# Output projection of the attention moved from the token tiles into the heads, in a transformer block on one core

## The chip, the core and the metric

The kernel runs on one core of a Trainium2 chip. The metric is the device time of one execution in microseconds; it is compared with the median of three runs of the kernel before, 3258.67 us (3257.95 to 3259.64).

## What is computed

The block has two halves, each behind a layernorm that is scaled and shifted per batch. Four batches of 2048 tokens with 512 channels; 16 heads of 32 channels, so 64 pairs of batch and head ("heads" below). In each head only the 409 queries with the largest norm attend; the output of all other tokens is zero in that head. Cut to what matters:

```
Q, K, V = proj(Wq, bq), proj(Wk, bk), proj(Wv, bv)      # 64 heads of 2048 x 32
_, top_idx = top_k(norm(Q), 409)
out_sel = softmax(Q[top_idx] @ K.T / sqrt(32)) @ V       # 409 x 32 per head
out_full = zeros(64, 2048, 32); out_full[:, top_idx] = out_sel
attn = reshape(out_full) @ Wo.T + bo                     # (4, 2048, 512)
x = x + ga * attn
h = layernorm(x) * (1 + cb) + sb
hq = fp4(h)                                              # blocks of 16: scale = max|h|/6, rounding to 8 levels
hid = fp4(silu(hq @ Wg.T) * (hq @ Wu.T))                 # 1408 wide
x = x + gb * (hid @ Wd.T)
```

`fp4` divides each block of 16 by its scale, rounds to the grid 0, 0.5, 1, 1.5, 2, 3, 4, 6 and multiplies by the scale again. Every product with a weight is done in three f16 matmuls (high by high, high by low, low by high), which keeps f32 accuracy.

## The kernel before

The program is written instruction by instruction: each engine (TensorE = PE, VectorE = DVE, ScalarE = ACT, GpSimd = POOL, SyncE = SP, which issues the plain DMAs) has its own list, executed in order, and semaphores tie the lists together. There are four stages: queries, keys and values (both before the change's main part), the attention (`attend`), and the feed-forward tiles (`feed_forward`).

**Attention.** `drive` runs 64 slots, one per head; the middle ones are a loop with two slots in its body. A slot has 8 steps k = 0..7. In every step PE computes the scores of 256 keys against 410 queries (`scores`, line 1614) into one pair of PSUM banks, ACT takes the exponential of them (`exponentials`, line 1517), and in the odd steps PE multiplies the exponentials of two earlier steps with the values (`weigh`, line 1625, f32). The next `scores` must wait for the exponential, since there is one pair of banks. Between them stand pieces for neighbouring heads: `scores_for_max` (line 1576) two heads ahead, whose maxima DVE takes (line 1412), `turn_queries` (line 1562), `rows`, `gather_last`, and `turn_output` for the head before. `divide` (DVE) divides by the sum of the exponentials, POOL's `scatter` adds the bias of the values and writes the 409 rows of 32 channels to DRAM with four indirect DMAs (`o_d`, line 1373), at the tokens' places. The rest of `o_d` is filled with zeros beforehand. POOL's list per head: cut the fetched queries, fetch the next ones (four indirect DMAs), scatter.

**Feed-forward.** 64 tiles of 128 tokens, one slot each, again a loop in the middle (four slots in its body). A slot t works on three tiles at once: the front of tile t+1 (attention output, residual, layernorm, `quantise_h`), the gate and up products of tile t (`gate_up`, three column chunks k of 512, 512 and 384, lines 2158 to 2160), and the down product of tile t-2 (`down`, lines 2180 to 2182). In the front, tile t+2 of `o_d` is turned (`turn_a`, 4 transposes, line 2131), split into a high and a low f16 part (`high_of_a` on ACT, `low_of_a` on DVE), and `attention_out` multiplies it with Wo in 12 matmuls (lines 2137 to 2139); `take_attention` (DVE) scales and adds `bo`. Then POOL does `residual` and `modulate`, DVE `moments`, `normalise`, `quantise_h`, POOL `scale_h`, and PE's `turn_x` (line 2146) turns the tile at the start of its slot into PSUM bank t0. ACT and DVE split it (`high_of_x`, `low_of_x`), which `gate_up` needs. `hidden` (DVE, line 1919) multiplies silu and up; `hidden_units` scales the 1408 columns to units of their blocks; `hidden_add` and `hidden_take` round by adding and subtracting a constant of the element's own exponent (`add_magic`: mask the exponent, `max(.,1)*ROUND`, add); POOL's `scale_hidden` and PE's `turn_hidden` (line 2170; its second chunk also uses bank t0) feed `down`.

**The seam.** The last heads and the first tiles are written out by hand in `last` and in the special cases `at(t, 0)` to `at(t, 2)` of the slots, and in POOL's list after its loop over the heads.

## Time and profile before

| | |
|---|---|
| median of three runs | 3258.67 us |
| the profiled execution, its own time | 3256.89 us |
| span of the profiled execution | 3255.0 us |
| busy: PE, DVE, ACT, POOL | 97%, 78%, 35%, 48% |
| mean granted PE clock | 0.989 of full speed |
| queries, keys and values | 0 to about 637 us |
| attention | about 637 to 1566 us |
| feed-forward | about 1566 us to the end |

The profile lists for one execution when each engine worked on what. The last 1.9 us of the execution's time lie outside the span. A busy PE row does not by itself show that PE is the limit, since matmuls overlap and their ends are modelled: what matters is the distance between the starts of neighbouring instructions, and whether an engine sat idle before one.

### The profile page before, as it was taken

To read this page: it belongs to the slowest core of one execution; us is meant where nothing else is said; L and a number is where in the kernel's file an instruction comes from. 1 tells how busy PE (TensorE), PEld (TensorE's weight loads), DVE (VectorE), ACT (ScalarE), POOL (GpSimd) and SP (SyncE) were. 2 spreads that over 40 slices of the span, in tenths; PEclk is the share of its full clock that TensorE was granted. 3 is DMA by queue.
4 is the path that set the end of the run, shared out by engine and by line. 5 is a ranking of instruction groups with operands and counts; after the bars stand their busy time and mean duration, and the time that the engine had idled before them with its cause. 6 is when DMAs were issued, how large, how long until landed. Compare 5 with 4: busy or idle time off the path is not lost.

```text
span 3255.0 us, 49640 instructions
## 1 busy us (share of the span) xinstructions
PE 3148.5 (97%) x16552; PEld 1459.3 (45%) x16552; DVE 2545.4 (78%) x3750; ACT 1141.7 (35%) x1588; POOL 1563.1 (48%) x1420
## 2 busy tenths in 40 slices
PE   7999999799999999999999999999999999999998
PEld 3543454333333333333455555555555555555554
DVE  4658976566666666666799989889999998899985
ACT  6853333366666666665211111111111111111111
POOL 3432224356666666663544444444444444444442
PEclk9999999899999999999999999999999999999999
DMA  6858849854333333324100010000000010000000
GB/s 237 285 174 250 220 137 251 204 174 142 86 103 106 86 116 95 84 78 126 42 30 30 29 32 32 29 31 30 29 29 29 32 32 29 30 31 29 29 20 17
DMA packets 238230, 290.81 MB, mean 89 GB/s; under 512 B 94648, under 2 KB 150328, under 8 KB 237384
## 3 DMA queue, kind: packets, MB, share of 16 engines
q1 hardware_dynamic: 221768, 283.07, 29.2%
q0 software_dynamic: 16384, 6.76, 1.0%
q8 instruction: 42, 0.69, 0.1%
q14 instruction: 36, 0.29, 0.0%
HBM read 169.36 MB, written 111.70 MB: 86 GB/s over the span
## 4 chain that ended last, share of the span: by engine, by line
PE 74%; ACT 2%; DVE 2%; issue 1%; POOL 1%; DMA 0%; SPq 0%; ACTq 0%; POOLq 0%; DVEq 0%
PE bank L1625 12%; PE pair L2158 9%; PE pair L2160 9%; PE pair L2159 9%; PE pair L1614 7%; PE pair L1576 5%; PE bank L2182 4%; PE bank L2180 4%; PE bank L2181 4%; ACT shared L1517 2%; PE pair L2137 2%; PE pair L2138 2%; PE pair L2139 2%; PE bank L2170 1%; PE pair L2170 1%
## 5 line engine op out<-in xcount | busy, mean ns | idle before, releaser
L1412 DVE TENSOR_REDUCE top<-pair 128x1 f32<-128x1024 f32 x378 | 451.0, 1221 | 219.2 <-PE pair L1576 219.2
L1517 ACT ACTIVATE shared<-pair,p_bias 128x820 f32<-128x820 f32 x512 | 483.3, 944 | 373.8 <-PE pair L1614 373.6
L2158 PE MATMUL pair<-gu,xT_hi 128*128 128x512 f16 (+1 forms) x1536 | 555.9, 362 | 4.1 <-DVE bridge L1919 2.1
L2160 PE MATMUL pair<-gu,xT_lo 128*128 128x512 f16 (+1 forms) x1536 | 555.8, 362 | 0.0
L2159 PE MATMUL pair<-gu,xT_hi 128*128 128x512 f16 (+1 forms) x1536 | 555.7, 362 | 0.0
L1625 PE MATMUL bank<-shared,bridge 128*33 128x410 f32 x2048 | 404.2, 516 | 0.0
L455 POOL DMA_INDIRECT q_sel<-q_d,chosen x256 | 247.3, 966 | 96.7 <-issue 80.6
L1614 PE MATMUL pair<-q_exp,bridge 98*128 98x410 f16 x1024 | 267.8, 343 | 25.9 <-ACT shared L1517 25.4
L1373 POOL DMA_INDIRECT o_d<-o_rows,chosen x256 | 250.1, 977 | 81.5 <-issue 64.2
L2180 PE MATMUL bank<-dn,bridge 128*128 128x512 f16 x704 | 268.4, 381 | 0.0
L2181 PE MATMUL bank<-dn,bridge 128*128 128x512 f16 x704 | 268.2, 381 | 0.0
L2182 PE MATMUL bank<-dn,bridge 128*128 128x512 f16 x704 | 267.9, 381 | 0.0
L2090 ACT ACTIVATE silu<-pair 128x512 f32<-128x512 f32 (+1 forms) x128 | 69.6, 544 | 510.7 <-PE pair L2160 510.7
L1576 PE MATMUL pair<-bridge,q_max 96*128 96x512 f16 x756 | 209.0, 386 | 17.6 <-DVEq L1458 15.2
L2160 PEld LDWEIGHTS pair<-gu,xT_lo 128*128 128x128 f16 x1536 | 150.4, 98 | 154.4 <-issue 0.8
L2158 PEld LDWEIGHTS pair<-gu,xT_hi 128*128 128x128 f16 x1536 | 150.4, 98 | 140.9 <-issue 4.0
L2159 PEld LDWEIGHTS pair<-gu,xT_hi 128*128 128x128 f16 x1536 | 150.4, 98 | 137.6 <-issue 0.8
L2021 POOL TENSOR_SCALAR f_rstd<-f_mv 128x1 f32<-128x1 f32 x64 | 87.0, 1359 | 219.4 <-DVE f_mv L1892 219.4
L2084 ACT ACTIVATE xT_hi<-pair 128x512 f16<-128x512 f32 x64 | 38.2, 597 | 437.6 <-PE pair L2146 437.6
L1625 PEld LDWEIGHTS bank<-shared,bridge 128*33 128x33 f32 x2048 | 98.1, 110 | 204.4 <-issue 204.1
L1614 PEld LDWEIGHTS pair<-q_exp,bridge 98*128 98x128 f16 x1024 | 64.4, 97 | 264.2 <-ACT shared L1517 233.0
L2038 POOL TENSOR_TENSOR bridge<-bridge,q_scale 128x1408 f32<-128x1408 f32 x64 | 165.8, 2590 | 24.8 <-DVE bridge L1804 17.5
(270 smaller groups left out, 6000.9 us busy)
## 6 DMA issues: line engine op xcount, KB each, us to landing
bridge<-k_d SPq DMA_DIRECT2D x384, 128.0 KB
v_d<-v SPq DMA_DIRECT2D x16, 1056.0 KB, 10.0
bridge<-v_d SPq DMA_DIRECT2D x64, 264.0 KB, 2.7
x<-in_x SPq DMA_DIRECT2D x16, 1024.0 KB, 8.8
q_d<-q SPq DMA_DIRECT2D x16, 1024.0 KB, 4.3
a_in<-o_d SPq DMA_DIRECT2D x64, 256.0 KB, 2.6
f_x<-in_x SPq DMA_DIRECT2D x64, 256.0 KB, 2.6
out<-shared SPq DMA_DIRECT2D x64, 256.0 KB, 2.0
```

The costliest lines, as they stand in the source:

```text
L1373: pool.indirect_dma_start(o_rows, bass.IndirectOffsetOnAxis(ap=con["chosen"][0:n, t, h:h + 1], axis=0), o_rows_of[u][0:n, t, :], None).the ...
L1412: ve.tensor_reduce(top[:, t, half:half + 1], ps[:, :, :].rearrange("p a n -> p (a n)"), AX.X, ALU.max, negate=True).then_inc(max_done, 1)
L1517: act.activation(p32[k % PB][:, :, :], ps_exp[:, :, 0:NQ], ACT.Exp, bias=con["p_bias"][:, 0:1], scale=scale).then_inc(p_done, 1)
L1576: last = pe.matmul(ps[:, s, :], q_max[u][:, t * P:(t + 1) * P], k_max[u][:, at:at + 512], start=True, stop=True)
L1614: last = pe.matmul(ps_exp[:, s, 0:NQ], k_exp[u][:, at:at + P], q_exp[u][:, :], start=True, stop=True)
L1625: last = pe.matmul(ps_out[at:at + VCOLS, 0:NQ], v_tok[u][:, t, :], p32[k % PB][:, s, :], start=k == 0, stop=k == STEPS - 1)
L2158: pe.matmul(o, xT_hi[:, c, :], w_hi[:, c, c0:c0 + n], start=c == 0, stop=False)
L2159: pe.matmul(o, xT_hi[:, c, :], w_lo[:, c, c0:c0 + n], start=False, stop=False)
L2160: last = pe.matmul(o, xT_lo[:, c, :], w_hi[:, c, c0:c0 + n], start=False, stop=c == KC - 1)
L2180: pe.matmul(ps_d[:, :], hT_hi[:, c, :], w_hi[:, c, :], start=c == 0, stop=False)
L2181: pe.matmul(ps_d[:, :], hT_hi[:, c, :], w_lo[:, c, :], start=False, stop=False)
L2182: last = pe.matmul(ps_d[:, :], hT_lo[:, c, :], w_hi[:, c, :], start=False, stop=c == FC - 1)
```

## The change

The projection with Wo is done per head. Since Wo acts on a head's 32 channels alone, the 409 rows of a head times 32 rows of Wo give 409 rows of 512 channels that are added to the tokens' rows. In each attention slot there are now:

- on DVE, behind the division: the bias of the values (scaled), the split into f16 parts side by side (`o_split`, 96 columns: high, low, high);
- on PE, `turn_back` (four transposes by matmul, into 96 x 410) at step 2, two slots behind the head's own; DVE copies it to SBUF (`take_back`);
- on PE, `project`: four matmuls, one for each 128 queries, at steps 5 and 7 (two heads back) and 1 and 3 (three heads back), 96 rows (high, low, high) against `wo_head` (high, high, low of Wo's rows), 512 columns;
- on ACT, `take_rows`: the 128 x 512 result is scaled into `o_tile`;
- on POOL, `scatter`: four indirect DMAs per head that add (compute_op add) rows of 512 channels, 2 KB each, to `o_d`. The rows of two heads can meet in one token, so the first DMA of a head waits until all of the head before have landed. POOL's scatter stands two heads later in its list than before. `o_d` is filled with `bo` instead of zeros.
- on SP, three loads of `wo_head` and one of the head's bias per head.

In the feed-forward `turn_a`, `high_of_a`, `low_of_a`, `attention_out` and `take_attention` are gone; `residual` reads `a_in` directly. The block scales are computed with a two-input instruction (a constant tile `least` as second input) in place of one with two constants. For the hidden units the mask of the exponents moves to the end of `hidden_units`, ACT multiplies by ROUND (`magic`), and `max` goes into the instructions that add and subtract. `turn_x(t+1)` stands inside `down(t-2)` and `low_of_x(t+1)` at the end of DVE's slot. The down weights lie where `o_tile` is, so they are loaded after the last scatter.

The diff, cut to its core:

```diff
@@ attend
+    BACK_AT = 2
+    PROJECT_AT = {5: (-2, 0, False), 7: (-2, 1, True), 1: (-3, 2, True), 3: (-3, 3, False)}
...
                 def scatter(h):
-                    u = h % 2
-                    pool.wait_ge(o_divided, h + 1)
-                    pool.tensor_tensor(o_rows_of[u][:, :, :], o_rows_of[u][:, :, :],
-                                       early["bv"][:, h % H * HD:(h % H + 1) * HD].unsqueeze(1).to_broadcast([P, QT, HD]),
-                                       ALU.add).then_inc(o_biased, 1)
...
                     for t in range(QT):
                         n = rows_of(t, TOP)
-                        pool.indirect_dma_start(o_rows, bass.IndirectOffsetOnAxis(ap=con["chosen"][0:n, t, h:h + 1], axis=0),
-                                                o_rows_of[u][0:n, t, :], None).then_inc(o_stored[u], 16)
+                        pool.wait_ge(o_taken, h * QT + t + 1)
+                        if t == 0:
+                            for k in range(QT):
+                                need(pool, o_stored[k], 16 * h)
+                            if h % H == 0:
+                                pool.wait_ge(o_zeroed, 16 * (L // N) * (h // H + 1))
+                        pool.indirect_dma_start(o_rows, bass.IndirectOffsetOnAxis(ap=token[0:n, t, h:h + 1], axis=0),
+                                                o_tile[h % 2][t][0:n, :], None, compute_op=ALU.add).then_inc(o_stored[t], 16)
...
-                    if h >= 4:
-                        scatter(h - 4)
+                    if h >= 6:
+                        scatter(h - 6)
...
+                def take_back(h, u, bank):
+                    ve.wait_ge(o_back, h + 1)
+                    need(ve, o_proj, h * QT - QT)
+                    ve.tensor_copy(oT[u][:, :], bank[0:KROWS, 0:NQ]).then_inc(o_back_taken, 1)
...
+                    ve.tensor_tensor(o_div[:, :, :], o_div[:, :, :], bv_head[u][:, :].unsqueeze(1).to_broadcast([P, QT, HD]),
+                                     ALU.add).then_inc(o_step, 1)
...
+                    ve.tensor_copy(o_split[:, :, :].rearrange("p t (k r) -> p t k r", k=3)[:, :, 0:3:2, :],
+                                   o_div[:, :, :].unsqueeze(2).to_broadcast([P, QT, 2, HD])).then_inc(o_step, 1)
...
+                    ve.tensor_tensor(o_split[:, :, HD:2 * HD], o_div[:, :, :], o_split[:, :, 0:HD], ALU.subtract).then_inc(o_cut, 1)
...
+                def take_rows(h, u, t, bank):
+                    n = rows_of(t, TOP)
+                    act.wait_ge(o_proj, h * QT + t + 1)
+                    need(act, o_stored[t], h * 16 - 16)
+                    act.activation(o_tile[u][t][0:n, :], bank[0:n, :], ACT.Copy, scale=1.0 / (W_UP * O_UP)).then_inc(o_taken, 1)
...
+                def project(h, u, t, bank, loaded, taken):
...
+                    need(pe, o_taken, taken)
+                    pe.matmul(bank[0:n, :], oT[u][:, t * P:t * P + n], wo_head[u][:, :], start=True, stop=True).then_inc(o_proj, 1)
@@ feed_forward
-        ve.tensor_scalar(sc[:, :], am[:, :], 1.0 / 6.0, 1e-12, ALU.mult, ALU.max).then_inc(step, 1)
+        ve.scalar_tensor_tensor(out=sc[:, :], in0=am[:, :], scalar=1.0 / 6.0, in1=least[:, 0:nb], op0=ALU.mult,
+                                op1=ALU.max).then_inc(step, 1)
...
+            ve.tensor_scalar(mg2[:, :].bitcast(I32), xn2[:, :].bitcast(I32), EXP_BITS, None, ALU.bitwise_and).then_inc(q2_step, 1)
...
         def hidden_add(t):
-            add_magic(ve, t, xn2, mg2, q2_step)
+            ve.wait_ge(q2_step, t * QS + 6)
+            ve.scalar_tensor_tensor(out=xn2[:, :], in0=mg2[:, :], scalar=ROUND, in1=xn2[:, :], op0=ALU.max, op1=ALU.add)\
+              .then_inc(q2_step, 1)
...
+        def magic(t):
+            act.wait_ge(q2_step, t * QS + 5)
+            act.activation(mg2[:, :], mg2[:, :], ACT.Copy, scale=ROUND).then_inc(q2_step, 1)
...
-        def attention_out(t):
-            pe.wait_ge(a_lo, t + 1)
-            for c in range(KC):
-                pe.matmul(ps_w[:, :], aT_hi[:, c, :], wo_hi[:, c, :], start=c == 0, stop=False)
-                pe.matmul(ps_w[:, :], aT_hi[:, c, :], wo_lo[:, c, :], start=False, stop=False)
-                last = pe.matmul(ps_w[:, :], aT_lo[:, c, :], wo_hi[:, c, :], start=False, stop=c == KC - 1)
-            last.then_inc(w_ready, 1)
...
-        def down(t):
+        def down(t, turn=None):
...
             for k, (c0, n) in enumerate(T2_CHUNKS):
+                if k == 2 and turn is not None:
+                    turn_x(turn)
```

What it moves, at two places. First PE's list in a middle slot of the attention, steps 0 to 3 (`q_exp` are the scores, `shared` the exponentials in `weigh`, `q_max` the scores for the maxima, `q_split` the turned queries). Before:

```order
L1614 MATMUL pair<-q_exp,bridge 128x410 x2
L1562 MATMUL bank<-ident,q_split 96x128 x3
L1562 MATMUL bank<-ident,q_split 96x26
L1576 MATMUL pair<-bridge,q_max 128x512 x4
L1614 MATMUL pair<-q_exp,bridge 128x410 x2
L1625 MATMUL bank<-shared,bridge 33x410 x4
L1614 MATMUL pair<-q_exp,bridge 128x410 x2
L1576 MATMUL pair<-bridge,q_max 128x512 x2
L1580 MATMUL pair<-bridge,q_max 26x512 x4
L1614 MATMUL pair<-q_exp,bridge 128x410 x2
L1625 MATMUL bank<-shared,bridge 33x410 x4
```

The same place after, from step 1 on:

```order
L1671 MATMUL pair<-q_exp,bridge 128x410 x2
L1682 MATMUL bank<-shared,bridge 33x410 x2
L1714 MATMUL bank<-wo_head,oT 128x512
L1682 MATMUL bank<-shared,bridge 33x410 x2
L1671 MATMUL pair<-q_exp,bridge 128x410 x2
L1631 MATMUL pair<-bridge,q_max 128x512 x2
L1635 MATMUL pair<-bridge,q_max 26x512 x4
L1704 MATMUL bank<-ident,o_split 96x128 x3
L1704 MATMUL bank<-ident,o_split 96x26
L1671 MATMUL pair<-q_exp,bridge 128x410 x2
L1714 MATMUL pair<-wo_head,oT 25x512
L1682 MATMUL bank<-shared,bridge 33x410 x4
```

Step 1 has one projection between the two halves of `weigh`, step 3 one (of only 25 queries) in front of it, and `turn_back` stands at the end of step 2. Steps 5 and 7 are like 3 and 1, with 128 queries each.

Second, DVE's list in a feed-forward slot, from `hidden` of the second chunk to the first instructions of the next slot (`q_amax` to `q_xn` are `quantise_h` or, with `bridge`, `hidden_units`; rows of the same kind within `quantise_h` are left out on both sides). Before:

```order
L1919 SCALAR_TENSOR_TENSOR bridge<-pair,silu 128x384
L1782 TENSOR_REDUCE q_amax<-bridge 128x88
L1785 TENSOR_SCALAR q_scale<-q_amax 128x88
L1787 RECIPROCAL q_inv<-q_scale 128x88
L1789 SCALAR_TENSOR_TENSOR bridge<-bridge,q_inv 128x1408
L1933 SCALAR_TENSOR_TENSOR bridge<-bank,shared 128x512
L1872 TENSOR_TENSOR xT_lo<-pair,xT_hi 128x512
L1925 SCALAR_TENSOR_TENSOR bridge<-bank,bridge 128x512
```

After:

```order
L2017 SCALAR_TENSOR_TENSOR bridge<-pair,silu 128x384
L1885 TENSOR_REDUCE q_amax<-bridge 128x88
L1888 SCALAR_TENSOR_TENSOR q_scale<-q_amax,f_least 128x88
L1891 RECIPROCAL q_inv<-q_scale 128x88
L1893 SCALAR_TENSOR_TENSOR bridge<-bridge,q_inv 128x1408
L2002 TENSOR_SCALAR bridge<-bridge 128x1408
L1975 TENSOR_TENSOR xT_lo<-pair,xT_hi 128x512
L2031 SCALAR_TENSOR_TENSOR bridge<-bank,shared 128x512
L2023 SCALAR_TENSOR_TENSOR bridge<-bank,bridge 128x512
```

The mask of the exponents (line 2002) now stands ahead of `low_of_x` (line 1975), and `low_of_x` ahead of `take_down` (line 2031).

## Rows read from the trace of the kernel before

**Rows 1.** Length; busy PE, PEld, DVE, ACT, POOL; PE clock, DMA share, GB/s.
```profile
1000.00:1400.00 400.00, 389.81 (x2181) 132.98 (x2178) 272.07 (x476) 246.94 (x307) 251.04 (x308) 1.00 0.34 95
1800.00:2200.00 400.00, 400.00 (x2093) 209.91 (x2091) 359.90 (x447) 65.22 (x123) 192.83 (x140) 1.00 0.09 30
```
**Rows 2.** Timeline of PE in a feed-forward slot: start, duration, line, idle in brackets.
```profile
1997.74 0.60 PE L2146 MATMUL pair<-ident,q_xq 128*128 128x128 f32 x4
1998.18 0.60 PE L2170 MATMUL bank<-ident,bridge 128*128 128x128 f32 x4
1998.62 0.38 PE L2137 MATMUL pair<-wo_hi,aT_hi 128*128 128x512 f16 x1
...
2001.20 0.60 PE L2170 MATMUL pair<-ident,bridge 128*128 128x128 f32 x4
...
2012.33 0.60 PE L2131 MATMUL pair<-ident,a_in 128*128 128x128 f32 x4
...
2016.67 0.38 PE L2180 MATMUL bank<-dn,bridge 128*128 128x512 f16 x1
...
2023.79 0.60 PE L2146 MATMUL pair<-ident,q_xq 128*128 128x128 f32 x4
```
**Rows 3.** Timeline of PE in an attention slot.
```profile
1015.43 0.52 PE L1614 MATMUL pair<-q_exp,bridge 98*128 98x410 f16 x2
...
1016.20 1.04 PE L1576 MATMUL pair<-bridge,q_max 96*128 96x512 f16 x4
1017.07 0.52 PE L1614 MATMUL pair<-q_exp,bridge 98*128 98x410 f16 x2
1017.52 1.57 PE L1625 MATMUL bank<-shared,bridge 128*33 128x410 f32 x8
1019.03 0.52 PE L1614 MATMUL pair<-q_exp,bridge 98*128 98x410 f16 x2
...
1020.66 0.52 PE L1614 MATMUL pair<-q_exp,bridge 98*128 98x410 f16 x2 [0.35 <-ACT shared L1517]
...
1029.76 0.52 PE L1614 MATMUL pair<-q_exp,bridge 98*128 98x410 f16 x2
```
**Rows 4.** ACT grouped by line: count | busy us, mean ns | idle before, releasers.
```profile
L1517 ACT ACTIVATE shared<-pair,p_bias 128x820 f32<-128x820 f32 x512 | 483.3, 944 | 373.8 <-PE pair L1614 373.6
...
L1066 ACT ACTIVATE v<-mm 128x512 f32<-128x512 f32 x64 | 38.0, 604 | 92.3 <-PE mm L1100 70.1 <-DMA v_d<-v 22.0
```
**Rows 5.** Timeline of ACT: a copy of 1408 columns.
```profile
615.02 1.37 ACT L1045 ACTIVATE f_row_hi<-f_quant 128x1408 f16<-128x1408 f32 x1
```
**Rows 6.** Timeline of DVE in a feed-forward slot.
```profile
2004.55 1.84 DVE L1798 TENSOR_SCALAR bridge<-bridge 128x1408 f32<-128x1408 f32 x1
...
2013.16 0.69 DVE L1919 SCALAR_TENSOR_TENSOR bridge<-pair,shared 128x512 f32<-128x512 f32 x1 [0.24 <-ACT shared L2090]
2013.77 0.68 DVE L1877 SCALAR_TENSOR_TENSOR aT_lo<-pair,aT_hi 128x512 f16<-128x512 f32 x1
2014.92 0.69 DVE L1782 TENSOR_REDUCE q_amax<-f_h 128x32 f32<-128x512 f32 x1 [0.47 <-POOL f_h L2027]
2015.64 1.83 DVE L1785 TENSOR_SCALAR q_scale<-q_amax 128x32 f32<-128x32 f32 x1
...
2020.88 0.55 DVE L1919 SCALAR_TENSOR_TENSOR bridge<-pair,silu 128x384 f32<-128x384 f32 x1
...
2023.11 0.20 DVE L1785 TENSOR_SCALAR q_scale<-q_amax 128x88 f32<-128x88 f32 x1
...
2025.63 0.68 DVE L1933 SCALAR_TENSOR_TENSOR bridge<-bank,shared 128x512 f32<-128x512 f32 x1
```
**Rows 7.** Timeline of DVE near the end: the mask of 1408 columns while POOL rests.
```profile
3200.61 0.88 DVE L1796 TENSOR_SCALAR bridge<-bridge 128x1408 int32<-128x1408 int32 x1
```
**Rows 8.** Timeline of POOL: the second and the fourth scatter DMA of a head.
```profile
1028.31 0.98 POOL L1373 DMA_INDIRECT o_d<-o_rows,chosen  x1 [0.30 <-issue]
...
1030.87 0.93 POOL L1373 DMA_INDIRECT o_d<-o_rows,chosen  x1 [0.30 <-issue]
```

More of the change, by code:

```diff
@@ L1856, in run @@
             load_a(2, 2)
-            drive(sp, slot, last, scattered)
+            drive(sp, slot, last)
             for u in range(2):
@@ L1960, in slot @@
                 ve.wait_ge(vec_in["gb"], 16)
-            else:
-                low_of_x(t)
             if has(t, -2):
                 low_of_hidden(t - 2, 0)
-            if has(t, 1):
-                take_attention(t + 1)
             if has(t, -2):
@@ L1986, in slot @@
             hidden_units(t)
+            if has(t, 1):
+                low_of_x(t + 1)
             if has(t, -2):
@@ L2000, in run @@
             drive(ve, slot, last)
-        return low_of_a, take_attention, moments, normalise, quantise_h, low_of_x, run
+        return hidden, moments, normalise, quantise_h, low_of_x, run
     def gpsimd(pool):
@@ L2209, in slot @@
             gate_up(t, 1)
-            if has(t, 2):
-                turn_a(t + 2, t4 + 2)
             gate_up(t, 2)
             if has(t, -2):
-                down(t - 2)
+                down(t - 2, t + 1 if has(t, 1) else None)
         def last():
```

335 lines of the change are left out of this document (195 added, 140 removed).

## Prediction, before the changed kernel was run

> **What bounds the kernel now.** I read the busy times by stage first. In the feed-forward stretch PE is busy 400.00 of 400 us and DVE 359.90; in the attention stretch PE 389.81, DVE 272.07, ACT 246.94, POOL 251.04 [rows 1]. The granted clock is 1.00 of full speed (2.4 GHz) in both, so it can give nothing back. Since a busy row is no proof, I then read PE's timeline. A feed-forward slot goes from 1997.74 to 2023.79, 26.05 us, with no idle time in brackets [rows 2]: the distance between starts is PE's own work. An attention slot goes from 1015.43 to 1029.76, 14.33 us [rows 3]. Its odd steps are PE's work too: scores at 1017.07, next scores at 1019.03, 1.96 us, without a gap. Its even steps take 1.64 (1015.43 to 1017.07; 1019.03 to 1020.66), and one of them ends in 0.35 us in which PE waits for ACT's exponential [rows 3], which takes 0.94 [rows 4]. So in both stages time is counted in matmuls on PE, save for small slack in the even steps.
>
> **What the feed-forward loses.** `turn_a` is 1997.74 to 1998.18 by its twin `turn_x`, 0.44 us. `attention_out` is 1998.62 to 2001.20, 2.58 us for 12 matmuls, 0.215 each [rows 2]. 3.02 us per tile, 64 tiles: **-194**. All of it was PE time without a wait, so all of it is gained as long as no other engine becomes late.
>
> By the Trainium skill, "TensorE: Matmul & The Clock Gate", section "Back-to-back issue gap", a stream of weight loads and 512-column matmuls sustains some 131 ns each. By that, an estimate, the twelve would be 1.6 us and the saving 64 x 2.0 = 129. Here the starts stand 0.215 us apart, so the trace does not agree, and the sum goes by the rows.
>
> **Is DVE late then?** DVE is the one near its limit: 359.90 of 400 is 23.4 us of the 26.05, and the new slot would be 26.05 - 3.02 = 23.03. It loses `take_attention` and `low_of_a` (0.68 each by its row), the 1408-column multiplication by ROUND (1.84), and `max` costs nothing extra. The scale instruction takes 1.83 for 32 columns where the same form on 88 takes 0.20 [rows 6]; the long one looks like waiting for something else, not like work. I take the two-input form at 0.24 with its distance. Together that is 4.8 us less, so DVE has 18.6 us of work in 23.0. What counts is the order, so I follow one chain. PE ends the gate and up products of the second chunk at 2012.33 [rows 2]; DVE's `hidden` starts 0.83 later, at 2013.16, `low_of_a` (now gone) at 2013.77. `quantise_h` takes 2014.92 to 2020.88, 5.96; without the slow scale (1.87 start to start, of which 0.24 stay) 4.33. `hidden` of the third chunk and `hidden_units` take 2020.88 to 2025.63, 4.75 [rows 6]; the mask, which needs their result, starts about 0.12 later than a free instruction would and costs 0.88 [rows 7], of which about 0.08 lie beside the next; `low_of_x` costs 0.68 by `low_of_a`, with 0.06 for its wait. Sum from PE's end of the second chunk: 0.83 + 0.61 + 4.33 + 4.87 + 0.80 + 0.74 = 12.18 us. PE meanwhile has: third chunk 2012.33 to 2016.67 less `turn_a` 0.44, 3.90; `down` 2016.67 to 2023.79, 7.12 [rows 2]; `turn_x` inside it 0.44, the first `turn_hidden` 0.44. Sum 11.90. Then the second `turn_hidden` needs bank t0, which `low_of_x` frees. So PE waits about 0.3 us per tile: slot 23.3; over some 61 tiles **+18**. Bounds: nothing, if DVE's overlaps are a little better; and the mask at twice its price (it shares its place with POOL's long instructions in the middle of the stage, while rows 7 shows it with POOL at rest) adds 0.9 per tile, 55 us.
>
> ACT's multiplication by ROUND has its nearest row in a copy of 1408 columns, 1.37 us [rows 5]. It runs behind the mask while DVE does `low_of_x` and the next slot's first work, and ACT is busy 65.22 of 400 us [rows 1], so it is hidden. Were it not, it would cost 1.37 a tile, 88 us, less the 0.68 of `low_of_x` beside it.
>
> **What the attention gains in work.** `project` is four matmuls of 512 moving columns, as `scores_for_max` is: 1016.20 to 1017.07 for four, 0.87 [rows 3]. They stand in the odd steps, where PE has no slack, so 0.87 per slot is the least. Three of them stand beside the f32 `weigh`; two scores of 410 columns would be 0.2175 x 410 / 512 x 2 = 0.35, but `weigh` starts 0.45 behind them (1017.07 to 1017.52) [rows 3], so I add 0.09 for each new change of type: 1.13 per slot. `turn_back` is four transposes, about 0.44 by `turn_x`, at step 2, where PE idles 0.35 [rows 3]: up to 0.1 is left over. `take_rows` is a copy of 128x512 out of PSUM, 604 ns [rows 4], four per slot; ACT has 246.94 / 400 x 14.33 = 8.85 us of work in a slot and gets 11.3 in 15.5. DVE has 9.75 and gets four small instructions (at most 0.68 each), 12.5. No engine passes PE. Sum 1.13 to 1.2 per slot, some 62 slots: **+72**. Bounds: 54 (0.87 each, nothing else) and, if each projection also delays the exponentials that a scores matmul waits for, 1.6, 100.
>
> **The scatter.** A scatter DMA is 0.98 on POOL, and one of 25 rows 0.93, each with 0.30 before it [rows 8]: the price hardly knows the rows, so I take 1.28 for rows of 2 KB that add, too. POOL has 251.04 / 400 x 14.33 = 9.0 us busy a slot and eight gaps of 0.30, 11.4; without the scatters 6.3, without the bias add too about 6. So a slot of 15.5 leaves 2.3 us for each scatter DMA. The transfers move 409 x 2 KB = 0.84 MB a slot; if adding means reading too, 2.5 MB at three passes. 95 GB/s are 0.34 of the engines' time [rows 1], so full would be 279 GB/s: 9.0 us more beside today's 4.9, 13.9 of 15.5. It fits, not by much.
>
> **The seam.** POOL's scatter stands two heads later, so behind the loop there are eight more scatter DMAs in front of the first tiles' residuals: 8 x 1.28 [rows 8], **+10**. Bounds 5 (half of it beside PE's last steps) and 30 (the landing of the last additions must be awaited before `a_in` and before the down weights come in). The first slot's fewer DMAs and the last tile's shorter tail change 1 or 2 us, against each other.
>
> **Sum** against the profiled execution: 3256.9 - 194 + 18 + 72 + 10 = 3163. The median of the runs is 1.8 above that execution, so **3164** us; 2.9% faster.
>
> **The rivals.**
>
> *The feed-forward slot follows DVE's chain.* For it: 12.18 against 11.90 is already on the wrong side, and each tenth that DVE loses there (a quantisation that comes later since POOL's `modulate` comes later, a mask beside POOL) is PE's. In the worst order `quantise_h` ends as late after the third chunk as now, 2020.88 - 2016.67 = 4.2 us; then units, mask and `low_of_x` follow, 4.2 + 4.87 + 0.80 + 0.74 = 10.6 against 7.12 + 0.88 = 8.0 of PE: 2.6 per tile, 157 us in place of 18. Against it: the 1.83 scale was the main lateness. Time 3200 to 3300. Chance 0.15.
>
> *The attention's slot is longer than its matmuls.* In the odd steps ACT now has the exponential and a 0.60 copy, 1.55 of 1.96; if the copy starts just ahead of the next exponential, scores, exponential and copy form a ring, and each of four steps gains up to 0.3 more. 16.2 us a slot, +0.75 x 62: about 3210. Chance 0.13.
>
> *The other side: the adding scatter.* One mechanism: a scatter DMA costs POOL, or its landing before the next head's first, more than the slot has. At s us for one, the slot is 6 + 4 s. Attention becomes limiting at s = 2.3; the kernel is slower than before when the slot takes about 17.1, since -194 + 18 + 10 = -166 over 62 slots is 2.7 more than 14.33: s = 2.8, or a head's additions landing over 12 us. At s = 3.0 the slot is 18.0: 3257 - 166 + 62 x 3.7 = 3320. For it: no row shows a DMA that adds, and 128 descriptors of 2 KB stand where 128 bytes were. Against it: 0.98 against 0.93. Chance 0.06.
>
> A page of the Trainium skill, "DMA: Bandwidth & Descriptors", section "Anatomy of one DMA", gives about 2.0 us and bytes / 436e3: 2.6 us to the landing of a 256 KB scatter, an estimate, which would fit between heads; no row of this case shows an adding one.
>
> *The adopted sum*, with its small terms off by a little: 0.64. The last 0.02: gains and losses cancel.
>
> **Range and chances.** The sum's own range: the DVE term 0 to 55, attention 54 to 100, seam 5 to 30, 3131 to 3225 at the extremes, which do not come together; with the rivals at 3200 to 3210 inside and what the saved DVE time may give beyond, 3128 to 3218 for 8 in 10. What a measurement can tell from no change is 0.2%, 6.5 us. Faster 0.92, same 0.02, slower 0.06.
>
> **What would show it.** Feed-forward slots of 23.3 us from `turn_x` to `turn_x`, with some 0.3 us of idle PE ahead of the second `turn_hidden`, released by DVE's `low_of_x`; no PE wait there means the mask is cheap. The scale at 0.2 instead of 1.83. Attention slots of 15.5, PE gap-free in the odd steps, `turn_back` in the old 0.35 gap; POOL scatter rows near 1.0. The prediction is wrong where a scatter row is over 2 us, or where PE's wait in a feed-forward slot is over 1 us.

## The result, and the profile after

The changed kernel takes 3300.71 us (median of 4 runs, 3296.10 to 3301.42), the kernel before in the same comparison 3259.01: ratio 1.0125, 95% interval 1.0108 to 1.0143. It is 1.3% slower where 2.9% faster was forecast. The profiled execution has a span of 3298.2 us, 43.2 more than before.

The busy times of the same two stretches as [rows 1]:

```profile
1000.00:1400.00 400.00, 399.76 (x2182) 133.91 (x2179) 281.51 (x534) 279.15 (x381) 279.89 (x255) 1.00 0.72 147
1800.00:2200.00 400.00, 374.94 (x1909) 191.59 (x1908) 323.09 (x415) 79.64 (x127) 208.62 (x143) 0.99 0.10 32
```

From the page, the shares of the chain that ended last, and the group of the adding scatters (count, busy us, mean ns, idle before):

```profile
PE 42%; DVE 22%; POOL 8%; issue 6%; DMA 1%; ACT 1%; POOLq 0%; DVEq 0%; SPq 0%; ACTq 0%
...
L1394 POOL DMA_INDIRECT o_d<-dn,token x256 | 400.8, 1566 | 251.1 <-ACT dn L1564 182.8
```

In the attention PE has no idle time left: 399.76 of 400. In the feed-forward, where PE was busy 400 of 400, it now idles 25 us in 400, and DVE's share of the last chain, 2% before, is 22%.

The starts of PE's own landmarks in both timelines divide the span (us):

| part | before | after | difference | forecast |
|---|---|---|---|---|
| to the first scores of the attention | 640.3 | 642.3 | +2.1 | 0 |
| to its last scores | 923.9 | 1013.0 | +89.1 | +72 |
| to the fourth `turn_x` | 68.9 | 77.6 | +8.7 | +10, less some 9 of saved work |
| 60 feed-forward slots | 1562.4 | 1506.2 | -56.2 | -164 |
| from the last `turn_x` to the end | 59.6 | 59.1 | -0.5 | some -3 |

The forecast's -194 + 18 is 2.74 us for each of the 60 slots and the rest in the first and last tiles. The slots' miss, 108 us, is four fifths of the whole miss of 137 us (43 slower in place of 94 faster).

PE's timeline in a feed-forward slot, the counterpart of [rows 2]:

```profile
1998.89 0.33 PE L2236 MATMUL pair<-gu,xT_hi 128*128 128x384 f16 x1
...
2007.97 0.61 PE L2224 MATMUL pair<-ident,q_xq 128*128 128x128 f32 x4
...
2010.36 0.60 PE L2248 MATMUL bank<-ident,bridge 128*128 128x128 f32 x4
2012.94 1.08 PE L2248 MATMUL pair<-ident,bridge 128*128 128x128 f32 x4 [1.98 <-DVE xT_lo L1975]
2013.82 0.63 PE L2236 MATMUL pair<-gu,xT_hi 128*128 128x512 f16 x1
2014.24 0.63 PE L2237 MATMUL pair<-gu,xT_hi 128*128 128x512 f16 x1
...
2016.62 0.38 PE L2237 MATMUL pair<-gu,xT_hi 128*128 128x512 f16 x1
2016.84 0.38 PE L2238 MATMUL pair<-gu,xT_lo 128*128 128x512 f16 x1
```

From the end of the second chunk's products, 1998.89, to where the second `turn_hidden` could start, 2010.36 + 0.44, PE needs 11.91 us: the forecast's 11.90. But it starts at 2012.94, released by `low_of_x`, after PE has rested 1.98 us and not 0.3. Behind this stop the matmuls start 0.43 apart in place of 0.22. The granted clock there:

```profile
2005.00:2010.00 5.00, 5.00 (x27) 2.47 (x26) 4.79 (x8) 0.60 (x1) 1.06 (x1) 1.00 0.00 0
2013.00:2016.00 3.00, 3.00 (x10) 1.56 (x11) 2.27 (x4) 1.67 (x3) 2.44 (x2) 0.50 0.00 0
```

0.50 is the lower of its two levels, 1.2 GHz, after some 2 us of rest; 2012.94 to 2016.38 then costs about 1.7 us more. It happens in 12 of the 60 slots, behind rests of 1.95 to 1.98 us; in 36 others PE rests 1.73 to 1.98 us (once 0.87) and the granted clock stays at 1.00.

DVE's and POOL's timelines of the same stretch, in order of time:

```profile
2000.43 2.59 POOL L2132 TENSOR_TENSOR bridge<-bridge,q_scale 128x1408 f32<-128x1408 f32 x1
2000.51 0.69 DVE L1885 TENSOR_REDUCE q_amax<-f_h 128x32 f32<-128x512 f32 x1
2001.23 1.84 DVE L1888 SCALAR_TENSOR_TENSOR q_scale<-q_amax,f_least 128x32 f32<-128x32 f32 x1
...
2012.20 0.68 DVE L1975 TENSOR_TENSOR xT_lo<-pair,xT_hi 128x512 f16<-128x512 f32 x1
...
2015.42 2.11 DVE L2006 SCALAR_TENSOR_TENSOR bridge<-bridge 128x1408 f32<-128x1408 f32 x1
2016.13 2.53 POOL L2111 TENSOR_TENSOR shared<-f_x,bridge 128x512 f32<-128x512 f32 x1
...
2018.70 0.69 DVE L1980 BATCH_NORM_STATS2 f_stats<-shared 128x6 f32<-128x512 f32 x1 [1.16 <-POOL shared L2111]
...
2025.45 2.59 POOL L2132 TENSOR_TENSOR bridge<-bridge,q_scale 128x1408 f32<-128x1408 f32 x1
...
2027.95 0.19 DVE L1888 SCALAR_TENSOR_TENSOR q_scale<-q_amax,f_least 128x32 f32<-128x32 f32 x1
```

The scale of 32 columns takes 1.84 us in its new two-input form as in the old one (1.83, [rows 6]), and ends at 2003.07, where POOL's multiplication of 1408 columns ends (2003.02). In the next slot it comes later, has 0.09 us in common with the same POOL instruction, and takes 0.19. The reduction between them lies wholly inside POOL's instruction and takes its plain 0.69. So one kind of DVE instruction waits for POOL and another does not. POOL waits as well: its addition at 2016.13 (1.26 where DVE leaves it alone) takes 2.53 and ends 1.1 after DVE's `hidden_add` (the row at 2015.42). The Trainium skill, "SBUF — State Buffer", section "Who interferes with whom", says which: a DVE instruction with two inputs in SBUF excludes a POOL instruction that reads SBUF, and so does a `tensor_scalar` in a mode that uses both ports; a reduction does not. By that rule the new form of the scale cannot help, since it trades one reason for the other. These rows agree for the scale, the reduction and POOL's addition; the prediction did not weigh it.

An attention slot on PE, the counterpart of [rows 3]:

```profile
1022.67 0.52 PE L1671 MATMUL pair<-q_exp,bridge 98*128 98x410 f16 x2
1023.12 0.88 PE L1682 MATMUL bank<-shared,bridge 128*33 128x410 f32 x4
1023.93 0.39 PE L1714 MATMUL bank<-wo_head,oT 96*128 96x512 f16 x1
1024.25 0.88 PE L1682 MATMUL bank<-shared,bridge 128*33 128x410 f32 x4
1025.07 0.52 PE L1671 MATMUL pair<-q_exp,bridge 98*128 98x410 f16 x2
...
1026.28 0.51 PE L1704 MATMUL bank<-ident,o_split 128*96 128x128 f16 x4
1026.72 0.52 PE L1671 MATMUL pair<-q_exp,bridge 98*128 98x410 f16 x2
1027.17 0.39 PE L1714 MATMUL pair<-wo_head,oT 96*25 96x512 f16 x1
1027.49 1.57 PE L1682 MATMUL bank<-shared,bridge 128*33 128x410 f32 x8
1028.99 0.52 PE L1671 MATMUL pair<-q_exp,bridge 98*128 98x410 f16 x2
```

Step 1 takes 2.40 us (1.96 before): the projection 0.32, and the split `weigh` 0.81 + 0.82 in place of 1.51. `turn_back` sits where PE had idled, and its step is 1.65. The slot is 15.77, without a wait.

### The profile page after: what moved, and what is told of

It reads as the page before. It is cut to its first block, busy times and chain, and to the rows that moved or that the text cites. A ratio compares the mean times of both kernels' runs of the same rounds, so it can differ in the third digit from the quotient of the medians.

```text
span 3298.2 us, 50101 instructions
## 1 busy us (share of the span) xinstructions
PE 3110.1 (94%) x16040; PEld 1392.6 (42%) x16040; DVE 2429.2 (74%) x3815; ACT 1329.3 (40%) x1844; POOL 1737.4 (53%) x1357
## 4 chain that ended last, share of the span: by engine, by line
PE 42%; DVE 22%; POOL 8%; issue 6%; DMA 1%; ACT 1%; POOLq 0%; DVEq 0%; SPq 0%; ACTq 0%
PE bank L1682 12%; PE pair L1671 7%; PE pair L1631 5%; DVE q_amax L1885 4%; PE pair L2238 4%; PE pair L2236 4%; PE pair L2237 4%; DVE q_scale L1888 3%; DVE bridge L1893 3%; DVE q_inv L1891 2%; DVE bridge L2017 1%; DVE q_xn L1893 1%; DVE q_xn L1904 1%; POOL f_rstd L2115 1%; POOL f_h L2119 1%
## 5 line engine op out<-in xcount | busy, mean ns | idle before, releaser
L2236 PE MATMUL pair<-gu,xT_hi 128*128 128x512 f16 (+1 forms) x1536 | 564.6, 368 | 4.1 <-DVE bridge L2017 2.3
L2237 PE MATMUL pair<-gu,xT_hi 128*128 128x512 f16 (+1 forms) x1536 | 564.5, 368 | 0.0
L2238 PE MATMUL pair<-gu,xT_lo 128*128 128x512 f16 (+1 forms) x1536 | 563.9, 367 | 0.0
L1394 POOL DMA_INDIRECT o_d<-dn,token x256 | 400.8, 1566 | 251.1 <-ACT dn L1564 182.8
L1682 PE MATMUL bank<-shared,bridge 128*33 128x410 f32 x2048 | 429.9, 520 | 0.0
L1631 PE MATMUL pair<-bridge,q_max 96*128 96x512 f16 x756 | 219.4, 386 | 18.0 <-DVEq L1493 15.2
L2126 POOL TENSOR_TENSOR q_xq<-q_xn,q_scale 128x512 f32<-128x512 f32 x64 | 68.3, 1068 | 230.5 <-DVE q_xn L1908 230.5
L1682 PEld LDWEIGHTS bank<-shared,bridge 128*33 128x33 f32 x2048 | 87.0, 110 | 169.6 <-issue 141.7
```

Of the source, the lines that this page charges most:

```text
L1394: pool.indirect_dma_start(o_rows, bass.IndirectOffsetOnAxis(ap=token[0:n, t, h:h + 1], axis=0), o_tile[h % 2][t][0:n, :], None, compute_op ...
L1631: last = pe.matmul(ps[:, s, :], q_max[u][:, t * P:(t + 1) * P], k_max[u][:, at:at + 512], start=True, stop=True)
L1682: last = pe.matmul(ps_out[at:at + VCOLS, 0:NQ], v_tok[u][:, t, :], p32[k % PB][:, s, :], start=k == 0, stop=k == STEPS - 1)
L2236: pe.matmul(o, xT_hi[:, c, :], w_hi[:, c, c0:c0 + n], start=c == 0, stop=False)
L2237: pe.matmul(o, xT_hi[:, c, :], w_lo[:, c, c0:c0 + n], start=False, stop=False)
L2238: last = pe.matmul(o, xT_lo[:, c, :], w_hi[:, c, c0:c0 + n], start=False, stop=c == KC - 1)
```

## Experiments

All but the thirteenth, which is the kernel before, are edits of the changed kernel. They ran in five groups, each on another chip and each beside the kernel before: it took 3258 us in runs 1 to 4 and 17 to 18, 3328 in 5 to 8, 3327 in 9 to 12 and 3289 in 13 to 16. The changed kernel itself was timed again only in the third and fourth group. Runs 1 to 4, 17 and 18 are therefore set against its first 3300.71 us, which is sound in so far as the kernel before took the same there within 1.2 us; all other times are compared within their group. A "stop" below is a rest of PE of more than 1 us in the attention; slots without one can be compared across the groups.

**1. The old form of the scale.**

```diff
-        ve.scalar_tensor_tensor(out=sc[:, :], in0=am[:, :], scalar=1.0 / 6.0, in1=least[:, 0:nb], op0=ALU.mult,
-                                op1=ALU.max).then_inc(step, 1)
+        ve.tensor_scalar(sc[:, :], am[:, :], 1.0 / 6.0, 1e-12, ALU.mult, ALU.max).then_inc(step, 1)
```

> One edit to the changed kernel: the block scales are computed again by the one-input instruction with two constants (line 1888). Theory A: in the feed-forward DVE and POOL cannot both use what they share, so the scale of 32 columns waits inside itself until POOL's multiplication of 1408 columns (line 2132) is over, whatever its form, as both forms have a second way into SBUF: its rows stay at 1.8 us in the slots where they overlap, 0.2 where they do not, and the time stays at 3300 us within 6. Rival B: the two-input form changed something after all (it removed a wait elsewhere, as its use in the change suggests): then the time rises by 10 us or more.

3292.95 us (3291.11 to 3293.92), ratio 1.0105 (1.0088 to 1.0122). The scale's rows are 1.83 or 0.18 as before, the slot 25.06 on average against 25.10. The form changes nothing in the wait. The 8 us are 2 more than I allowed; the slots give 60 x 0.04 = 2.5 of them, so that the old form is if anything the better one, and where the others come from was not followed.

**2. Maxima and inverse scales in PSUM.**

```diff
+    am1p, in1p = (banks[0][:, 0, k * (D // BLK):(k + 1) * (D // BLK)] for k in range(2))
...
-            block_units(ve, t, D, h, am1, sc1, in1, xn1, q1_step, lambda: need(ve, q1_done, t))
+            am, inv = (am1, in1) if isinstance(t, int) and t < 4 else (am1p, in1p)
+            block_units(ve, t, D, h, am, sc1, inv, xn1, q1_step, lambda: need(ve, q1_done, t))
```

> One edit to the changed kernel: for the tokens' tiles from the fifth on, the block maxima (input of the scale) and the inverse scales (input of the product) of quantise_h lie in PSUM, in a bank that is free in this stage. So the scale and the product have one input in SBUF in place of two. Theory A (the second SBUF input is what collides with POOL): the scale takes 0.2 us instead of 1.84 everywhere, the chain to low_of_x is 1.1 to 1.6 us shorter per tile, slots of 23.6 to 24.0 instead of 25.1 on average, time about 3235 us (3215 to 3250). Rival B (the instruction waits for POOL for another reason, its output or its place): 1.84 stays, and the time stays within 6 us of 3300.

3216.39 us (3215.58 to 3218.27), ratio 0.9872 (0.9856 to 0.9889): 84 us less than the changed kernel, 1.3% faster than the kernel before, and inside the 3215 to 3250 of theory A. DVE and POOL, in order of time:

```profile
2009.88 2.59 POOL L2134 TENSOR_TENSOR bridge<-bridge,q_scale 128x1408 f32<-128x1408 f32 x1
...
2010.71 0.19 DVE L1889 SCALAR_TENSOR_TENSOR q_scale<-pair,f_least 128x32 f32<-128x32 f32 x1
2010.93 0.36 DVE L1892 RECIPROCAL pair<-q_scale 128x32 f32<-128x32 f32 x1
2011.33 0.69 DVE L1894 SCALAR_TENSOR_TENSOR q_xn<-f_h,pair 128x512 f32<-128x512 f32 x1
2012.05 0.70 DVE L1901 TENSOR_SCALAR q_magic<-q_xn 128x512 int32<-128x512 int32 x1
```

Scale, reciprocal and product now run inside POOL's instruction (to 2012.47) at 0.19, 0.36 and 0.69. The first that waits is the mask at 2012.05 (0.70 in place of 0.43), a `tensor_scalar` with one input and one constant. The slot is 23.77, 1.33 less; 60 x 1.33 = 80 of the 84. This edit takes the collision away without touching the amount of work, and it carries the case: for the two-input form the wait is the second input from SBUF, not the instruction, its size or its output, which still lies in SBUF.

**3. `low_of_x` ahead of the mask.**

```diff
             hidden_units(t)
             if has(t, 1):
                 low_of_x(t + 1)
+            hidden_mask(t)
```

(`hidden_mask` is the instruction that ended `hidden_units`.)

> One edit to the changed kernel: low_of_x stands ahead of the mask of the exponents on DVE instead of behind it. Theory A (PE's wait of 1.98 us ends with DVE's chain, in which the mask is 0.8): the wait before the second turn_hidden falls to about 1.2, slots 0.6 to 0.8 shorter, time 3301 - 60 x 0.7 = about 3259 us (3250 to 3270). Rival C (what comes behind is set by ACT's multiplication, which now starts 0.6 later, and pushes everything that it pushes back): no gain, 3295 to 3310.

3293.44 us (3291.54 to 3295.40), ratio 1.0111 (1.0094 to 1.0128). PE's wait for `low_of_x` falls to 1.06, and a new wait of 0.36 to 0.50 for POOL's `scale_h` stands ahead of `turn_x`; the slot is 25.04. Theory A's gain (3250 to 3270 us) did not come: rival C, that something pushes back, is right in kind, and the time is 1.6 us under its 3295.

**4. `low_of_x` inside `hidden_units`.**

```diff
+        if between is not None:
+            between()
         ve.wait_ge(step, done[2])
         ve.scalar_tensor_tensor(out=blocks(xn[:, :]), in0=blocks(src[:, :]), scalar=sign * TIE_DOWN,
```

> One edit to the changed kernel: low_of_x stands inside hidden_units, behind the reciprocal and ahead of the product of 1408 columns. Theory A: the chain to low_of_x loses 1.62 of the product and 0.89 of the mask, 2.5 us, more than PE's wait of 1.98; PE waits no longer, no drop of its clock follows, and the slot is PE's own work, 23.05 to 23.4: time 3301 - 60 x 1.9 = about 3190 us (3180 to 3205). Rival C (the next lateness, ACT's multiplication or DVE's total work, takes over): slots of 24 or more, 3230 and above.

3289.82 us (3288.40 to 3290.17), ratio 1.0098 (1.0081 to 1.0115). Theory A's 3190 did not come, rival C's slot of 24 or more did. PE's wait for `low_of_x` is gone altogether, and the slot is 24.97: in its place PE waits 1.14 us for `hidden` and 0.36 to 0.50 for POOL's `scale_h`. DVE's timeline shows what sets the slot then:

```profile
1963.76 0.69 DVE L2025 SCALAR_TENSOR_TENSOR bridge<-bank,bridge 128x512 f16<-128x512 f32 x1 [1.33 <-ACT bridge L2184]
...
1967.74 0.69 DVE L1982 BATCH_NORM_STATS2 f_stats<-x 128x6 f32<-128x512 f32 x1 [1.16 <-POOL x L2111]
...
1971.05 0.55 DVE L1988 TENSOR_SCALAR f_h<-x,f_mv,f_rstd 128x512 f32<-128x512 f32 x1 [0.77 <-POOL f_rstd L2117]
...
1974.54 0.69 DVE L1885 TENSOR_REDUCE q_amax<-f_h 128x32 f32<-128x512 f32 x1 [1.28 <-POOL f_h L2121]
1975.26 1.84 DVE L1888 SCALAR_TENSOR_TENSOR q_scale<-q_amax,f_least 128x32 f32<-128x32 f32 x1
```

DVE waits once for ACT and three times for POOL, and POOL's work there waits for DVE: a ring, that is waits of engines for each other that close from slot to slot, of 25 us beside the one through PE. Two limits lay 0.1 us apart, so undoing the first alone gives next to nothing; that the second experiment gives 80 us fits, since the wait of the scale lies in both.

**5 and 6. Both edits; then the second ring shortened.** The fifth is 2 and 4 together. The sixth adds two moves: POOL's multiplication by `ga` ahead of `result`, and ACT's splits ahead of its multiplication by ROUND.

```diff
+            if has(t, 1):
+                gain(t + 1, t4 + 1, b1)
             if has(t, -3):
                 result(t - 3, t4 + 1)
             if has(t, 1):
-                residual(t + 1, t4 + 1, b1)
+                add(t + 1, t4 + 1)
...
-            if not at(t, 1):
-                magic(t - 1)
             if has(t, -2):
                 high_of_hidden(t - 2, 0)
                 high_of_hidden(t - 2, 1)
+            if not at(t, 1):
+                magic(t - 1)
```

> The edits of the second and the fourth experiment together (maxima and inverse scales in PSUM, low_of_x inside hidden_units). Theory D, formed from the fourth: two rings of nearly the same length bound the feed-forward slot, PE with DVE's chain to low_of_x (25.1 us in the changed kernel) and DVE with POOL and ACT (24.9 to 25.0: waits of 1.33 for ACT, 1.16 and 0.77 and 1.28 for POOL, and 1.84 in the scale). PSUM takes 1.4 from both, the move takes 2.5 from the first alone: slots of 23.5, by 0.2 to 0.3 better than the second experiment's 23.77, about 3200 us (3190 to 3208). Rival: the gains of the two add up, 84 + 11, for 3206 or more, as if there were no rings; or PE's own 23.05 is reached, 3172.

> The fifth with the second ring shortened: POOL multiplies the attention by ga ahead of the result of tile t-3 instead of behind it, and ACT splits the hidden units' two chunks ahead of its multiplication by ROUND. Theory D: the waits of DVE for ACT (1.33) and for POOL's residual (1.16) shrink, the slot falls from 23.5 to PE's own 23.1: about 25 us less than the fifth, 3175 us (3165 to 3185). Rival: DVE's hidden_add and POOL's addition still exclude one another, so the residual is not earlier and the slot stays within 0.1 of the fifth's.

3382.18 us (ratio 1.0171, 1.0140 to 1.0202) and 3315.06 us (0.9956, 0.9938 to 0.9974), on a chip with a slower attention (below). The feed-forward's slots are 24.10 and 23.02. The fifth's is longer than the second's 23.77 where theory D had it 0.2 to 0.3 shorter: with the scale repaired, moving `low_of_x` forward costs 0.33 a slot. The trace shows where: `low_of_x` now stands ahead of the mask, so ACT's multiplication and its splits come later, and DVE waits 1.33 us for the splits where it waits 0.73 in the second run. So there are two rings, as theory D has it, but the second one was taken too short by 0.6. The sixth is 67 us under the fifth where 25 was expected, because the fifth was longer; its slot is the forecast one. PE is busy there without a gap, at the 23.03 that the prediction worked out as PE's own work. Of the two waits that its edit was to shrink, the one for ACT is gone, and the one for POOL's residual is still 1.17; what each of its two moves gives alone was not run.

**7. Projections ahead of `weigh`.** At steps 1 and 7 `project_in_turn` stands ahead of both halves.

```diff
                         if k == 1 and has(i, -1):
+                            project_in_turn(i, u, k)
                             weigh(i - 1, 1 - u, STEPS - 2, None)
-                            project_in_turn(i, u, k)
                             weigh(i - 1, 1 - u, STEPS - 1, None)
```

> One edit to the changed kernel: the projections of steps 1 and 7 stand ahead of both halves of weigh (between f16 and f32 matmuls once) instead of between them. Theory E: each f32 matmul behind an f16 one costs some 0.1 us more, so the two steps lose 0.2 each: slots of 15.35 instead of 15.77, time lower by 25 us (15 to 30), 3275. Rival: the projection then waits for ACT's copy out of the same bank, and step and time stay as they are within 6 us.

3458.71 us (ratio 1.0394, 1.0374 to 1.0413). The changed kernel has no time in this group, so the time tells nothing alone; the attention's slots without a stop, of which there are four, are 15.36 to 15.42 against 15.77. The expected slot of 15.35 came.

**8. Scatters that write instead of adding.** `compute_op` is left out.

> One edit to the changed kernel: the scatter DMAs write instead of adding, so that each token keeps only the last head's rows (the sum over heads is left out). It prices the adding: if 1.57 us on POOL (1.0 before) comes from adding, the rows fall to 1.0; if it comes from rows of 2 KB, they stay at 1.5 to 1.6. In either case the time stays within 6 us of 3300, since PE has no wait in the attention; only the seam, where the second of two heads waits 3.7 us for the landing of the one before, may give 1 to 3 us.

One execution: 3388.11 us beside 3328 for the kernel before. POOL's rows, grouped by line:

```profile
L1394 POOL DMA_INDIRECT o_d<-dn,token x256 | 253.2, 989 | 487.1 <-ACT dn L1564 443.3 <-issue 24.8 <-DMA vec_sb<-mod_d 12.7
```

0.99 us: rows of 2 KB cost POOL no more than rows of 128 B, adding costs 0.58. From 1000 to 1400 us the packets of the queue for the indirect DMAs took 41.4% of the DMA engines for 22.37 MB in the changed kernel and 14.8% for 20.49 MB here, 2.6 times less per byte. The attention has stops without the adding too, but it is shorter: 1106.1 us against 1160.2 and 1164.7 in the fifth and sixth run on the same chip, which have the changed kernel's attention. Only 1 to 3 us, in the seam, had been expected.

**9 to 12. The same kernels beside the changed one.** The ninth is the changed kernel, the tenth the sixth, the eleventh the sixth with the seventh's edit; the twelfth is the eleventh with `scale_h(2)` moved between the last two scatters.

```diff
                 scatter(BH - 2)
+                f_scale_h(2)
                 scatter(BH - 1)
```

> The changed kernel without an edit, beside the next three and the kernel before on one chip: in the last call the attention's slots were 17 to 20 us long in some and 15.4 or 15.8 in others, on a chip where the kernel before took 3328 us as well, so the times of that call cannot be set against those of the first. If the chip is like the first: 3300 us, attention slots of 15.77, feed-forward slots of 25.10 on average.

> The sixth experiment again (maxima and inverse scales in PSUM, low_of_x inside hidden_units, multiplication by ga ahead of the result, ACT's splits ahead of its multiplication). Feed-forward slots of 23.02 without any wait of PE, as the sixth showed: 60 slots less 2.08 each are 125 us under the changed kernel, 3175 us (3168 to 3182).

> The tenth and the seventh together: the projections of steps 1 and 7 ahead of weigh as well. The seventh's undisturbed slots were 15.36 to 15.42 against 15.77: 0.4 x 61 = 24 us under the tenth, 3151 us (3145 to 3160). If the rival of the seventh holds (a wait for ACT's copy takes the place): within 6 us of the tenth.

> The eleventh with one step of the seam moved: POOL scales tile 2 (scale_h(2)) between the scatters of the last two heads instead of behind both. In the changed kernel PE waits 5.6 us for it and then 1.5 us for the hidden units' scale, which stays behind the last scatter. Theory F: the first wait goes and comes back in part as the second, net 1.5 to 5 us: 3148 us; rival: the load of f_x, for which POOL waits 8.8 us just behind, ends last anyway, and nothing changes.

3447.59, 3317.71, 3335.83 and 3337.58 us; ratios 1.0369 (1.0338 to 1.0399), 0.9964 (0.9950 to 0.9979), 1.0031 (1.0013 to 1.0050), 1.0042 (1.0015 to 1.0069). Tenth less ninth: -130 (expected -125). Eleventh less tenth: +18, where -24 was expected. In the twelfth PE's first wait, 6.5 us in the eleventh, is gone, and the second has grown from 1.47 to 5.74: the three slots of the seam took 72.2 us against 72.7, which is nearly the rival's nothing. (In the changed kernel's first trace PE's two waits are 5.58 and 1.47.) PE's timeline in the ninth's attention shows the stops:

```profile
1217.34 0.52 PE L1671 MATMUL pair<-q_exp,bridge 98*128 98x410 f16 x2
...
1218.54 0.60 PE L1631 MATMUL pair<-bridge,q_max 96*128 96x512 f16 x2
1220.20 2.36 DVE L1439 TENSOR_REDUCE top<-pair 128x1 f32<-128x1024 f32 x2 [3.12 <-PE pair L1631]
1220.23 0.94 ACT L1552 ACTIVATE shared<-pair,p_bias 128x820 f32<-128x820 f32 x1 [3.00 <-remote]
1221.23 0.53 PE L1671 MATMUL pair<-q_exp,bridge 98*128 98x410 f16 x2 [2.09 <-ACT shared L1552]
```

ACT's exponential, for which PE waits, starts at 1220.23 after 3.00 us of rest, and DVE's next reduction at 1220.20 after 3.12, both with their matmuls long started. The slots are 15.8 to 21 us long (one 22.7), and in heads 8 to 60 step 0 takes 3.5 us on average in place of 1.64, step 1 2.9 in place of 2.4.

The busy times of the whole attention, in the changed kernel's first trace and in the ninth (columns as in [rows 1]):

```profile
642.30:1655.30 1013.00, 1002.86 (x5429) 334.62 (x5428) 706.50 (x1334) 695.97 (x944) 677.93 (x620) 0.99 0.71 148
642.20:1797.10 1154.90, 1053.20 (x5428) 337.44 (x5426) 707.82 (x1334) 692.86 (x944) 678.03 (x620) 0.96 0.64 130
```

Of the 142 us more, PE rests 92. The other 50 are busy time for the same number of matmuls, at a mean granted clock of 0.96 in place of 0.99: many of the stops are followed by a stretch at half clock.

**13 to 16. Where the kernel before loses there.**

> The kernel before without an edit, for its trace on this chip. If the chip is like the first: 3259 us, attention slots of 14.33, feed-forward slots of 26.05. If it is like that of the last two calls: 3327 us, with all of the 70 us in the attention, as stops of about 2 us in every second slot, and the feed-forward at 26.05; rival: the loss is spread over the stages.

> The changed kernel without an edit, as the measure of the two beside it: 3300 us on a chip like the first, 3448 on one like the second.

> The kernel of the sixth and tenth runs (the ring shortened, feed-forward slots of 23.02): 125 us under the changed kernel on either chip, 3175 on the first, 3318 on the second.

> The kernel of the eleventh run (projections of steps 1 and 7 ahead of weigh as well): on a chip like the first 24 us under the fifteenth, 3151 us; on one like the second again some 15 us above it, since there the stops, not PE's work, set the slot.

3288.93, 3410.77, 3289.38 and 3316.60 us, against 3288.82 for the kernel before; ratios of the last three 1.0374 (1.0343 to 1.0406), 1.0006 (0.9994 to 1.0018), 1.0090 (1.0060 to 1.0120). Fifteenth less fourteenth: -121 (expected -125). Sixteenth less fifteenth: +27 (expected some +15). The kernel before loses all of it in the attention: 955.2 us from its first to its last scores against 923.9 on the first chip, in steps 1 and 6 (2.17 and 1.91 on average against 1.96 and 1.68), as smaller and more frequent rests than I expected. 27 of its 31 us more are rests of PE, and its mean granted clock there stays at 0.99. The changed kernel's attention takes 1124.7 there against 1013.0: 76 us more of rest, and a clock of 0.97.

**17 and 18. The two best kernels, on a chip like the first.**

> The kernel of the sixth run (the ring shortened). On a chip like the first, where the kernel before takes 3259 us: 3175 us (3168 to 3182), 2.5% under it.

> The kernel of the eleventh run (projections of steps 1 and 7 ahead of weigh as well). On a chip like the first: attention slots of 15.36 to 15.4, 24 us under the seventeenth, 3151 us (3145 to 3160). On a chip with stops: 15 to 30 us above the seventeenth.

3170.55 us (3164.62 to 3172.22), ratio 0.9735 (0.9719 to 0.9751), and 3145.60 us (3144.28 to 3149.25), ratio 0.9660 (0.9644 to 0.9676). The eighteenth's busy times, and a step 1 on PE:

```profile
1000.00:1400.00 400.00, 399.75 (x2234) 141.93 (x2232) 287.76 (x546) 279.65 (x390) 285.66 (x261) 1.00 0.73 150
1800.00:2200.00 400.00, 400.00 (x2083) 208.02 (x2082) 329.11 (x452) 89.50 (x139) 227.76 (x157) 1.00 0.11 35
```

```profile
1013.60 0.52 PE L1671 MATMUL pair<-q_exp,bridge 98*128 98x410 f16 x2
1013.99 0.39 PE L1714 MATMUL bank<-wo_head,oT 96*128 96x512 f16 x1
1014.31 1.57 PE L1682 MATMUL bank<-shared,bridge 128*33 128x410 f32 x8
1015.82 0.52 PE L1671 MATMUL pair<-q_exp,bridge 98*128 98x410 f16 x2
```

Step 1 is 2.22 in place of 2.40, the slot 15.42 in place of 15.77, and the eighteenth is 25.0 us under the seventeenth. On this chip it beats both given kernels: 3.4% under the one before, and 155 us under the changed one's 3301. On the two chips with stops on which it ran, the same kernel was 0.3% and 0.9% slower than the one before (eleventh and sixteenth run).

## Why the prediction was wrong

**What bounds the kernel, and the work removed: right.** PE's own work in the new feed-forward slot was forecast at 23.03; the sixth run has 23.02, with no wait.

**"I take the two-input form at 0.24": the step that failed.** The prediction saw that 1.83 looked like waiting, and then let the wait go with the form of the instruction. It measured 1.80 to 1.88 from start to start in 48 of the 60 slots. In the chain of 12.18 us this is +1.64; the rest of the chain was off by 0.2 (`hidden` to reduction 0.79 in place of 0.61). 14.05 us against PE's 11.91 is the wait of about 2. The row to see it was in the trace of the kernel before, on POOL beside the scale of [rows 6], which ends at 2017.47:

```profile
2014.85 2.59 POOL L2038 TENSOR_TENSOR bridge<-bridge,q_scale 128x1408 f32<-128x1408 f32 x1
```

The wait ended with POOL's instruction, at 2017.44, and the first experiment shows that both forms have it. The second, which takes only the second SBUF input away, gets 80 of the slots' 108 us back. The other 28 are the 0.47 us by which its slot of 23.77 is over the forecast 23.3; PE still rests 0.41 to 0.66 for `low_of_x` there.

**The rival "the feed-forward slot follows DVE's chain" is what came,** at 25.10 on average; its band of 3200 to 3300 was missed by 0.7 us. It had a chance of 0.15, too little for 0.28 us between two chains of 12. The prediction also followed one chain alone. The second ring, over POOL and ACT, is 24.97 in the fourth run; shortening only the first, as that run does, gives 11 us. In it lies another collision of two SBUF inputs (`hidden_add` with POOL's addition) and ACT's multiplication by ROUND, costed at nothing with "so it is hidden": it stands ahead of the splits for which DVE waits 1.33 us.

**The clock: a term that was not in the sum, and costs nothing here.** The 12 slots of 26.90 with the lower clock are each followed by one of 23.39, since PE's lateness brings the scale behind POOL's instruction: 25.15 on average, as the other 36 (25.07). That the two cancel is luck.

**Attention +72: right mechanism, size 89.** It is PE's work as forecast. Splitting `weigh` costs 0.12 each time beside the projection's 0.32, 1.44 per slot in place of 1.13 to 1.2. The seventh and the eighteenth run show 0.35 of it as a matter of place. The scatter's price of 1.28 was 1.87 with its gap (adding +0.58), under the 2.3 at which it would have counted; the other side's rival, POOL at 2.8 and more, did not come. The DMA engines' share, worked out as 13.9 us of a slot of 15.5, was 0.72 of it, 11.4 us. **The seam** was +9 where +1 (10 less 9 of saved work) was forecast, so that its own term is some 18 in place of 10, inside its bounds; its waits are for POOL behind the scatters, as said.

**Open:** the stops in the attention on some chips. The trace names no engine as the releaser of ACT ("remote"), ACT and DVE start again in the same 0.03 us, and the kernel before rests more there as well, only in shorter pieces. They don't come from the adding alone, but it has a part in them: without it PE rests 20 us less than in the fifth run on the same chip and is busy 35 us less, at a clock of 0.98 in place of 0.95. A rival that no run tests is the scatter itself: in the ninth run 52 of PE's 57 rests of over 1 us begin while POOL is in a scatter DMA (POOL is in one or between two for some 40% of a slot), in the eighth, without the adding, 10 of 49; which of the two is cause is not shown. Each chip was met once, so that the chip makes the difference is likely and not shown either. Why the changed kernel has longer stops was not found, and on such chips the projections' better place costs 18 to 27 us instead of giving 25.

## What to carry to other kernels

A small instruction whose duration ends with another engine's points to a collision, and its form is changed only after asking which operand collides; moving a small operand to PSUM is a cheap way out. Before costing a wait at nothing, follow every ring through the slot, not only the one through the engine that bounds: here two limits of 25.1 and 25.0 us hid one another, and a repair of the first alone looked useless. Where f32 and f16 matmuls alternate, count the changes of type, and put the odd matmul where one is already paid.

## What the runs showed of the hardware

- DVE instructions with two SBUF inputs (also of 32 columns) waited for the end of a POOL instruction that reads SBUF, up to 1.6 us; with one input in PSUM they ran beside it (0.19 against 1.84). A `tensor_scalar` with its one input in SBUF waited too (1.83 for the scale, 0.70 in place of 0.43 for the mask); a reduction did not (0.69).
- An indirect DMA cost POOL 0.99 us for rows of 2 KB, as for rows of 128 B; adding made it 1.57, and the DMA engines' time per byte 2.6 times as long.
- In the changed kernel's feed-forward, 12 of 48 rests of PE of up to 1.98 us were followed by some 3 us at half clock.
- The kernel before took 3258, 3289 and 3327 us on different chips, the changed one 3301, 3411 and 3448. In the profiled executions the difference lies in the attention: 923.9 and 955.2 us before, 1013.0, 1124.7 and 1154.9 after, in part through the clock that falls behind longer rests. A change should be timed on more than one chip before it is called a gain.
